# The opening of a four-layer kernel on one core: matmuls that nobody reads, rows issued by two engines, shared weights in half pieces

## Chip, cores and metric

The program runs on one core of a Trainium2 chip. The metric is the device time of one execution in microseconds. All 16 sequences of the batch are computed in one launch.

## The reference

Sixteen sequences x of 256 tokens and 256 features go through four residual layers:

```python
x = x + linear(x, weight[subject], bias[subject])                  # L0
x = x + zX * lap_x(x) + zY * lap_y(x) + zR * x * (1 - x)           # L1, 3-point differences, mirrored edges
x = x + attention(x, side, length)                                 # L2
x = x + expert_mix(x, label)                                       # L3
```

L2 has 16 heads of 16 features. Its queries come from a second sequence `side`, the keys and values from x (masked by a length), and each query has one more score and value, its own, from `side`; an output projection Wo follows. L3 runs three two-layer ReLU networks of width 1024 on all tokens: two shared ones (`swi`, `swo`) and one chosen by the label (`wi`, `wo`). Their outputs are added with softmax weights that a small gate network computes from the first token.

## The kernel before

**Engines and lists.** Each engine runs its own program. What it does in which order is written out by hand as a list of names; a name such as `S3` or `kp` is a stage, and semaphores bind the stages of different engines together. `PE_BODY`, `ACT_BODY`, `DVE_BODY`, `POOL_BODY` and `SP_BODY` are one turn of the loop over sequences. A turn works on several sequences at once: the scores of one (`S`, `E`), the early layers of the next, and the experts (`H`, `P`) of the one before. `OPEN_PE`, `OPEN_ACT`, `OPEN_DVE`, `OPEN_POOL` and `OPEN_SP` (lines 114 to 135) are the opening, which fills this pipeline: it carries sequence 0 up to the experts' input and through its 16 heads, and sequence 1 (names ending in `.1`) up to its rows. Then the loop starts.

**Precision.** Values in fp32 are split into a high part (ScalarE copies it to the matmul's format) and a low part (the rest, subtracted by VectorE or GpSimd). A product is three matmuls: high with high, high with low, low with high (lines 631 to 633). A 256 by 256 projection is 12 matmuls of 128 by 128 weights and 256 columns. For the scores, q and k are split into three bf16 parts each, and copied by DMA into `q_rows` and `k_rows`, where the parts of one head lie stacked on the partitions: six bands of 16 rows each for q and for k, 128 KB per band, and a mask row that comes from memory (`place`, line 481). TensorE then gets a head's score in one product.

**The stages by name.** `x1` is L0 (12 matmuls with the subject's weight, which SP loads after it has read the subject number); `x1_parts` splits its result, `beside` (in the stage `x1` of GpSimd, line 1334) adds the two neighbours of each token, `react` is the reaction term, `lap` the difference along features (four matmuls with `lap_mats`), `x2_parts` splits the result of L1. `q`, `kp`, `ks`, `vs`, `vp`, `self` are the projections of the side sequence and of x with three of the four matrices of `wqkvo` (in `raw`, split by `lin0` to `lin3` into `lin_hi` and `lin_lo`) and the own scores. `qa`, `qb`, `kq`, `k3` make the second and third parts. `S0` to `S15` compute the scores of a head with queries on the partitions, only to find their maxima (VectorE, line 1125). `m0` and `m1` turn the maxima of eight heads round, and a DMA puts them into `q_rows` (line 516). `E0` to `E15` compute the scores again with keys on the partitions; ScalarE takes two exponentials of each (lines 966 and 970), VectorE or GpSimd makes the low part (1145, 1378), and TensorE multiplies with the values three heads later (`attend`, lines 693 and 694). `half`, `norm` and `att` divide the sums, `aT` transposes them, `wo` is the output projection. `H` and `P` are steps of the two expert layers. The S and E heads and the projections share two PSUM banks in the order in which they are listed, so a stage waits until the one two places ahead in the list has been read.

**The shared weights.** `swi` and `swo` are 4 MB in eight pieces of 512 KB. Each has to be loaded to a place that is free, split into `exp_hi` by ScalarE and into `exp_lo` by VectorE (pieces 0 and 1) or GpSimd (2 to 7), and its place can then be used again. The places are written in one list:

```python
STAGES = ["e_out", "gate1", "raw0", "raw1", "e_out", "gate1", "e_out", "gate1"]
```

Pieces 4 and 5 therefore wait for the split of 0 and 1, pieces 6 and 7 for that of 4 and 5, which in the opening's lists comes late. The gate's own weights go to `gate1` after that.

**Warm matmuls.** Before the first load has landed, TensorE runs 16 matmuls on `q_rows` that nobody reads (`warm`, line 845), after VectorE has set `q_rows`.

## Time and profile before

| | before |
|---|---|
| time, median of 3 runs | 1043.14 us (1041.8 to 1044.29) |
| the profiled execution's own time | 1044.92 us |
| its span in the profile | 1043.1 us |
| TensorE busy | 979.5 us (94%) |
| VectorE busy | 777.6 us (75%) |
| ScalarE busy | 688.6 us (66%) |
| GpSimd busy | 618.6 us (59%) |

Times in the profile are microseconds from the start of the span. PE is TensorE, PEld its weight loads, DVE is VectorE, ACT ScalarE, POOL GpSimd, SPq the sequencer of SyncE that issues DMAs. A line number is one of the kernel's. "<-" behind idle time names what ended it. The granted clock is TensorE's, as a share of 2.4 GHz. The end of a matmul is modelled, so the pace of a series of matmuls is read from their starts.

### The profile page before, as it was taken

What the parts mean: (1) busy time and instruction counts of PE and PEld (TensorE: products, weight loads), DVE (VectorE), ACT (ScalarE), POOL (GpSimd) and SP (SyncE); (2) the same over time, 40 slices, a digit from 0 to 9 for tenths busy, and PEclk for the clock granted to TensorE, in tenths of its full rate; (3) what the DMA queues carried; (4) which work ended last, traced back from release to release, by engine and by line L of the source; (5) the groups of instructions that cost most, each with busy time, mean ns of one, the idle gap of its engine ahead of it and who ended that gap; (6) DMA issues with size and microseconds to landing.
All of it is one profiled execution on the core that took longest, in us unless ns stands there. A gap on an engine that the chain in (4) does not pass through costs nothing.

```text
span 1043.1 us, 27678 instructions
## 1 busy us (share of the span) xinstructions
PE 979.5 (94%) x9504; PEld 921.1 (88%) x9504; DVE 777.6 (75%) x1553; ACT 688.6 (66%) x1435; POOL 618.6 (59%) x545
## 2 busy tenths in 40 slices
PE   7567999999999999999999999999999999999886
PEld 6256999999999999899999999999999999999886
DVE  5755778787877878787787878778777878778643
ACT  4365676858667685867767586776768587676641
POOL 4467566747565664756576575657657565665540
PEclk9567999999999999999999999999999999999998
DMA  5515343152425325142522514342341524243110
GB/s 145 148 42 109 95 90 94 45 115 63 61 82 97 85 56 117 51 71 81 91 81 66 113 44 85 87 70 81 76 106 41 102 81 61 81 87 66 43 51 11
DMA packets 91387, 82.68 MB, mean 79 GB/s; under 512 B 11972, under 2 KB 90852, under 8 KB 91364
## 3 DMA queue, kind: packets, MB, share of 16 engines
q1 hardware_dynamic: 91364, 82.38, 34.5%
q8 instruction: 14, 0.23, 0.1%
q14 instruction: 9, 0.07, 0.0%
HBM read 52.59 MB, written 4.20 MB: 54 GB/s over the span
## 4 chain that ended last, share of the span: by engine, by line
PE 58%; issue 11%; DVE 8%; ACT 7%; SPq 6%; POOL 6%; DMA 4%; ACTq 0%; DVEq 0%; POOLq 0%
PE out L631 6%; PE out L632 6%; PE out L633 6%; PE hid L631 5%; PE front L751 5%; PE hid L632 4%; PE hid L633 4%; PE front L631 4%; PE front L633 4%; PE front L632 4%; PE front L738 3%; DMA raw<-in_wo 3%; PE pv L693 3%; PE pv L694 2%; ACT prob_hi L970 2%
## 5 line engine op out<-in xcount | busy, mean ns | idle before, releaser
L1378 POOL TENSOR_TENSOR prob_lo<-prob,prob_hi 128x512 f16<-128x512 f32 x144 | 173.4, 1204 | 115.3 <-ACT prob_hi L970 115.3
L631 PE MATMUL hid<-x_hi,exp_hi 128*128 128x256 f32 x768 | 230.7, 300 | 2.0 <-DVE x_lo L1205 2.0
L631 PE MATMUL out<-hid_hi,exp_hi 128*128 128x256 f32 x768 | 227.3, 296 | 4.1 <-DVE hid_lo L1209 3.5
L632 PE MATMUL hid<-x_lo,exp_hi 128*128 128x256 f32 x768 | 216.6, 282 | 0.0
L633 PE MATMUL hid<-x_hi,exp_lo 128*128 128x256 f32 x768 | 215.9, 281 | 0.0
L632 PE MATMUL out<-hid_lo,exp_hi 128*128 128x256 f32 x768 | 214.9, 280 | 0.0
L633 PE MATMUL out<-hid_hi,exp_lo 128*128 128x256 f32 x768 | 214.7, 280 | 0.0
L1317 POOL TENSOR_TENSOR exp_lo<-raw,exp_hi 128x512 fp32r<-128x512 f32 x128 | 169.8, 1342 | 68.4 <-ACT exp_hi L986 68.4
L1125 DVE TENSOR_REDUCE s_max<-front 128x2 f32<-128x512 f32 x256 | 168.9, 687 | 53.4 <-PE front L738 51.2
L966 ACT ACTIVATE prob<-front 128x512 f32<-128x512 f32 x256 | 153.4, 600 | 51.0 <-PE front L751 51.0
L1008 ACT ACTIVATE hid_hi<-hid 128x512 fp32r<-128x512 f32 x192 | 114.6, 597 | 106.1 <-PE hid L633 104.3
L1209 DVE SCALAR_TENSOR_TENSOR hid_lo<-hid,hid_hi 128x512 fp32r<-128x512 f32 x192 | 130.5, 680 | 52.3 <-ACT hid_hi L1008 50.1
L631 PEld LDWEIGHTS out<-hid_hi,exp_hi 128*128 128x128 f32 x768 | 144.8, 188 | 8.1 <-DVE hid_lo L1209 4.2
L631 PEld LDWEIGHTS hid<-x_hi,exp_hi 128*128 128x128 f32 x768 | 145.1, 189 | 4.7 <-DVE x_lo L1205 2.2
L632 PEld LDWEIGHTS hid<-x_lo,exp_hi 128*128 128x128 f32 x768 | 145.5, 189 | 0.0
L632 PEld LDWEIGHTS out<-hid_lo,exp_hi 128*128 128x128 f32 x768 | 145.2, 189 | 0.0
L633 PEld LDWEIGHTS hid<-x_hi,exp_lo 128*128 128x128 f32 x768 | 144.9, 189 | 0.0
L633 PEld LDWEIGHTS out<-hid_hi,exp_lo 128*128 128x128 f32 x768 | 144.6, 188 | 0.0
L970 ACT ACTIVATE prob_hi<-front 128x512 f16<-128x512 f32 x240 | 143.8, 599 | 0.0
L751 PE MATMUL front<-q_rows,k_rows 100*128 100x256 bf16 x512 | 125.2, 280 | 11.3 <-ACT prob_hi L970 7.6
L1145 DVE TENSOR_TENSOR prob_lo<-prob,prob_hi 128x512 f16<-128x512 f32 x112 | 92.6, 827 | 17.0 <-ACT prob_hi L970 16.0
L738 PE MATMUL front<-k_rows,q_rows 97*128 97x256 bf16 x512 | 90.6, 285 | 13.2 <-DVE s_max L1125 7.0
(174 smaller groups left out, 2273.1 us busy)
## 6 DMA issues: line engine op xcount, KB each, us to landing
raw<-in_wi SPq DMA_DIRECT2D x64, 256.0 KB, 3.5
raw<-in_wo SPq DMA_DIRECT2D x64, 256.0 KB, 2.9
q_rows<-w_raw SPq DMA_DIRECT2D x80, 128.0 KB, 3.6
k_rows<-x1T SPq DMA_DIRECT2D x48, 128.0 KB, 4.4
k_rows<-x_raw SPq DMA_DIRECT2D x48, 128.0 KB, 5.5
x_raw<-in_x SPq DMA_DIRECT2D x16, 256.0 KB, 2.9
s_raw<-in_side SPq DMA_DIRECT2D x16, 256.0 KB, 3.7
w_raw<-in_w SPq DMA_DIRECT2D x16, 256.0 KB, 2.8
```

The costliest lines, as they stand in the source:

```text
L631: nc.tensor.matmul(acc, w_hi, a_hi, start=first, stop=False)
L632: nc.tensor.matmul(acc, w_hi, a_lo, start=False, stop=False)
L633: return nc.tensor.matmul(acc, w_lo, a_hi, start=False, stop=last)
L738: last = nc.tensor.matmul(psum[:, t * S:(t + 1) * S], q_rows[0:ROWS_MAX, h, t * P:(t + 1) * P], k_rows[0:ROWS_MAX, h, :], start=True, stop ...
L751: last = nc.tensor.matmul(psum[:, k * S:(k + 1) * S], k_rows[0:ROWS_EXP, h, k * P:(k + 1) * P], q_rows[0:ROWS_EXP, h, :], start=True, stop ...
L966: last = nc.scalar.activation(prob[:, h % NPROB, :], psum[:, :], ACT.Exp, scale=SCALE)
L970: last = nc.scalar.activation(prob_hi[:, h % NPROB, :], psum[:, :], ACT.Exp, scale=SCALE)
L1008: nc.scalar.activation(hid_hi[:, s % 2, :], hid_bank[s % 2][:, :], ACT.Relu).then_inc(hid_hi_done, 1)
L1125: nc.vector.tensor_reduce(s_max[:, :, h:h + 1], psum, AX_X, ALU.max).then_inc(freed["S"], 1)
L1209: nc.vector.scalar_tensor_tensor(hid_lo[:, s % 2, :], hid_bank[s % 2][:, :], 0.0, hid_hi[:, s % 2, :].bitcast(F32), ALU.max, ALU.subtract) ...
L1317: nc.gpsimd.tensor_tensor(lo, source, hi.bitcast(F32), ALU.subtract).then_inc(w_split, 1)
L1378: nc.gpsimd.tensor_tensor(prob_lo[:, h % NPROB, :], prob[:, h % NPROB, :], prob_hi[:, h % NPROB, :], ALU.subtract).then_inc(prob_split_poo ...
```

## The change

The loop's lists stay as they are. In the opening:

- TensorE's list gets 19 `fill` entries, 93 matmuls of 256 columns with `lap_mats` into `hid1`, which nobody reads; `warm` has 20 matmuls instead of 16, reads `v_cols` and so waits for GpSimd's first memset instead of VectorE's. E0 to E3 move in between S13, S14 and S15, x1.1 and m1 move later.
- The first k copies (`k0`, three DMAs) are issued by ScalarE instead of SP; SP's order becomes q0, q1, mask row, q2, k1, k2.
- The first loads go out as subject, x, w0, small, s instead of x, subject, s, w0, small.
- A shared piece is loaded, and split, in two halves of 256 KB, each with its own place; there are ten such places (x3T, x3_kept and the ends of e_out and gate1 are new). Pieces 2 and 3 are loaded ahead of load.1, 4 to 7 right behind m0. VectorE splits three pieces (0, 1, 5), GpSimd five. The matmuls in H0, H4, P0, P4 and P8 wait for the counts that this gives, by constants; that is three waits more per sequence.
- lin0 to lin3 are all split by GpSimd, in halves, with one semaphore. `beside` of sequence 0 is VectorE's. k3 goes ahead of shared0 on VectorE, and GpSimd waits for the first half's maxima (`maxima`) before it splits the inputs of sequence 1. The other lists are rearranged to fit.

```diff
 OPEN_PE = list(opening("""
-warm x1 bias_q lap q bias_k kp ks vs vp self
-S0 S1 S2 S3 S4 S5 S6 S7 S8 m0 S9 S10 S11 S12 S13 S14 S15 E0 E1 m1 x1.1 E2 E3 E4 E5 E6 q.1 E7 lap.1 E8 E9 E10 E11 kp.1 E12 E13 E14 E15
-pvend vs.1 aT ks.1 wo vp.1 self.1
+warm x1 bias_q fill14 lap q bias_k kp ks vs vp self fill4
+S0 S1 fill4 S2 S3 fill4 S4 S5 fill4 S6 S7 S8 fill10 m0 S9 S10 fill4 S11 S12 fill8 E0 E1 S13 S14 fill2 E2 E3 S15 x1.1 E4 fill3 E5 fill3
+m1 E6 q.1 E7 fill3 lap.1 E8 fill3 E9 fill3 E10 fill3 E11 kp.1 E12 fill3 E13 fill3 E14 fill3 E15 fill6
+pvend vs.1 fill6 aT ks.1 wo vp.1 self.1
 """))
 OPEN_ACT = list(opening("""
-x_parts s_parts w_parts lin0 x1_parts react lin1 lin2 x2_parts q qa lin3 shared0 kp qb kq ks shared1 vs vp x2b
-w_parts.1 x_parts.1 s_parts.1 m0 shared2 E0 E1 m1 shared3 E2 x1_parts.1 react.1 E3 E4 E5 E6 q.1 E7 qa.1 E8 x2_parts.1 E9 E10 E11 kp.1
-E12 E13 E14 E15 qb.1 kq.1 shared4 aT vs.1 ks.1 shared5 x3_parts vp.1 x2b.1 shared6 shared7
+x_parts w_parts s_parts lin0 x1_parts react lin1 lin2 x2_parts q qa lin3 kp qb k0 kq ks vs shared0 vp shared1 x2b
+shared2 shared3 w_parts.1 x_parts.1 m0 s_parts.1 E0 E1 E2 E3 E4 E5 m1 x1_parts.1 react.1 E6 q.1 E7 shared4 qa.1 E8 x2_parts.1
+E9 E10 E11 kp.1 E12 E13 E14 E15 qb.1 kq.1 shared5 shared6 aT vs.1 ks.1 shared7 x3_parts vp.1 x2b.1
 """))
 OPEN_DVE = list(opening("""
-memsets x_lo s_lo w_lo laps x_parts x1 lin0 x1_parts bias_q react lap x2_parts setup bias_k kp shared0 k3 vp self shared1
-S0 S1 S2 S3 S4 S5 S6 S7 S8 S9 S10 S11 S12 x_parts.1 S13 S14 S15 x1.1 E1 x1_parts.1 react.1 E3 E5 lap.1 E7 x2_parts.1 half E11 kp.1
-E13 E15 att k3.1 aT wo x3_parts vp.1 self.1
+memsets x_lo w_lo s_lo laps x_parts x1 beside x1_parts react bias_q lap setup x2_parts bias_k kp k3 shared0 vp self shared1
+S0 S1 S2 S3 S4 S5 S6 S7 S8 S9 S10 S11 S12 x_parts.1 S13 S14 E1 S15 x1.1 E3 x1_parts.1 react.1 E5 E7 lap.1 x2_parts.1 half E11 kp.1
+E13 E15 att k3.1 aT shared5 wo x3_parts vp.1 self.1
 """))
 OPEN_POOL = list(opening("""
-memsets x1 lin1 lin2 qa lin3 qb ks vp w_parts.1 x_parts.1 s_parts.1 shared2 E0 x1.1 E2 shared3 E4 E6 m1 E8 E9 qa.1 E10 E12 norm E14
-qb.1 shared4 ks.1 shared5 vp.1 shared6 shared7
+memsets lin0 lin1 qa lin2 qb ks vp lin3 shared2 maxima w_parts.1 x_parts.1 s_parts.1 E0 E2 x1.1 shared3 E4 E6 m1 E8 shared4 E9 qa.1
+E10 E12 norm E14 qb.1 ks.1 vp.1 shared6 shared7
 """))
 OPEN_SP = list(opening("""
-mask q0 k0 q1 k1 mask_row q2 k2 load.1 shared2 shared3 shared4 shared5 m0 m1 wi_load E15 kp.1 k3.1 shared6 shared7 gates
+mask q0 q1 mask_row q2 k1 k2 shared2 shared3 load.1 m0 shared4 shared5 shared6 shared7 m1 wi_load E15 kp.1 k3.1 gates
 """))
...
-STAGES = ["e_out", "gate1", "raw0", "raw1", "e_out", "gate1", "e_out", "gate1"]
+STAGES = [("e_out", 0, 1), ("gate1", 0, 1), ("raw", 0, 1), ("x3", 0, 1), ("raw", 2, 3), ("ends", 0, 1), ("e_out", 0, 1), ("gate1", 0, 1)]
 SHARED = len(STAGES)
-SHARED_DVE = 2
+SHARED_DVE = 3
...
-WARM = 16
+WARM = 20
...
             def load_shared(n):
...
+                e, part = n // 4, n % 2
+                for m, dest in enumerate(staged(n)):
+                    if n % 4 < 2:
+                        columns = slice(m * F // 2, (m + 1) * F // 2)
+                        sp.dma_start(dest, swi[e, part * P:(part + 1) * P, columns]).then_inc(shared_in[n], 16)
+                    else:
+                        chunks = F // 4
+                        at = slice((2 * part + m) * chunks, (2 * part + m + 1) * chunks)
+                        sp.dma_start(dest.rearrange("p (f d) -> p f d", d=D),
+                                     swo[e, at].rearrange("(f p) d -> p f d", p=P)).then_inc(shared_in[n], 16)
...
-                    wait(sp, w_split, PARTS, i, 4 - SHARED_DVE if isinstance(i, int) and i == 0 else SHARED_POOL)
+                    wait(sp, w_split, PARTS, i, 3 if isinstance(i, int) and i == 0 else SHARED_POOL)
...
+            sp.dma_start(subject_sb[:, :], subject).then_inc(choice_in, 16)
             load_x(0)
-            sp.dma_start(subject_sb[:, :], subject).then_inc(choice_in, 16)
-            load_s(0)
             sp.wait_ge(choice_in, 16)
             load_w0(chooser(subject_sb, 0, w0.shape[0]))
             load_small(0, chooser(subject_sb, 0, w0.shape[0]))
+            load_s(0)
...
                 if s == 0:
                     wait(pe, x3_split, 1, j, 1)
+                    pe.wait_ge(shared_split_dve, 2)
+                elif s == STEPS:
                     pe.wait_ge(shared_split_dve, SHARED_DVE)
-                    pe.wait_ge(w_split, 4 - SHARED_DVE)
-                elif s == STEPS:
-                    pe.wait_ge(w_split, SHARED_POOL)
+                    pe.wait_ge(w_split, 4)
...
                 if s == 0:
                     wait(pe, logits_read, 1, j, 1)
+                    pe.wait_ge(w_split, 2)
                 elif s % STEPS == 0:
                     wait(pe, e_out_done, NE, j, e)
+                    pe.wait_ge(w_split, SHARED_POOL)
...
-                pe.wait_ge(q_rows_set, 1)
+                pe.wait_ge(rows_set, 1)
+                plane = v_cols[:, 0, :, :].rearrange("p h w -> p (h w)")
                 for _ in range(WARM):
-                    nc.tensor.matmul(front_bank[0][:, 0:S], q_rows[0:ROWS_MAX, 0, 0:P], q_rows[0:ROWS_MAX, 1, :], start=True, stop=True)
+                    nc.tensor.matmul(hid_bank[1][:, 0:S], plane[:, 0:P], plane[:, 0:S], start=True, stop=True)
+
+            def fill(count):
+
+                pe.wait_ge(consts_set, 1)
+                for _ in range(count):
+                    nc.tensor.matmul(hid_bank[1][:, 0:S], lap_mats[:, 0:P], lap_mats[:, :], start=True, stop=True)
...
+                elif name == "k0":
+                    act.wait_ge(rows_set, 3)
+                    act.wait_ge(k_part_done, C)
+                    place(act, k_rows, K_BANDS, k_parts, 0, k_placed)
...
+                elif name == "beside":
+                    dve.wait_ge(freed["x1"], 1)
+                    ends = x1T[:, :, 1:S - 1:S - 3]
+                    nc.vector.tensor_tensor(beside[:, :, 1:S - 1], x1T[:, :, 0:S - 2], x1T[:, :, 2:S], ALU.add)
+                    nc.vector.tensor_tensor(beside[:, :, 0:S:S - 1], ends, ends, ALU.add).then_inc(beside_done, 1)
...
+                elif name == "wo":
+                    dve.wait_ge(w_split, 2)
+                    stage(name, seq)
...
+                elif name == "maxima":
+                    pool.wait_ge(max_split, 1)
```

## Rows read from the trace of the kernel before

**Rows 1.** Stretches of the whole run; columns: busy time and count by engine, granted clock, DMA.

```profile
0.00:55.00 55.00, 36.65 (x170) 26.17 (x170) 32.83 (x64) 22.08 (x41) 23.57 (x23) 0.78 0.51 139
55.00:110.00 55.00, 40.33 (x331) 34.94 (x330) 30.46 (x52) 31.32 (x60) 38.59 (x33) 0.72 0.45 102
...
170.00:1043.00 873.00, 843.33 (x8412) 803.53 (x8410) 667.66 (x1343) 592.67 (x1245) 519.13 (x457) 1.00 0.33 75
```

**Rows 2.** The chain of waits in order of time, its start: start us, us, what.

```profile
1.22 2.32 DMA subject_sb<-in_subject
...
4.51 2.66 DMA w_raw<-in_w
```

**Rows 3.** Timeline of TensorE: start us, us, what, idle time before it.

```profile
14.62 0.55 PE L716 MATMUL front<-x_hi,lap_mats 128*128 128x256 f32 x1 [1.60 <-DVE x_lo L1069]
...
16.46 0.41 PE L632 MATMUL front<-s_lo,lin_hi 128*128 128x256 f32 x1
16.68 0.41 PE L633 MATMUL front<-s_hi,lin_lo 128*128 128x256 f32 x1
...
18.17 1.70 PE L841 MATMUL pv<-vec_sb,raw 128*128 128x2 f32 x8
...
24.25 0.28 PE L631 MATMUL front<-s_hi,lin_hi 128*128 128x256 f32 x1
24.37 0.28 PE L632 MATMUL front<-s_lo,lin_hi 128*128 128x256 f32 x1
```

**Rows 4.** Timeline of SP's DMA queue: first k0 copy group, last row copy.

```profile
23.65 1.83 SPq L485 DMA_DIRECT2D k_rows<-x1T  x3
...
30.79 0.60 SPq L485 DMA_DIRECT2D k_rows<-x_raw  x1
```

**Rows 5.** The chain of waits, the last row copy's way.

```profile
30.79 3.96 DMA k_rows<-x_raw
```

**Rows 6.** Stretch in which the last row copies move.

```profile
30.00:32.00 2.00, 0.00 (x0) 0.00 (x0) 1.12 (x1) 0.00 (x0) 2.00 (x2) 0.73 1.06 138
```

**Rows 7.** Timeline of TensorE, VectorE and ScalarE in the S heads.

```profile
34.99 1.01 PE L738 MATMUL front<-k_rows,q_rows 97*128 97x256 bf16 x4 [6.23 <-DMA k_rows<-x_raw]
...
35.61 5.48 DVE L1125 TENSOR_REDUCE s_max<-front 128x2 f32<-128x512 f32 x8 [4.49 <-PE front L738]
...
41.33 1.14 DVE L1134 TENSOR_SCALAR m_parts<-s_max 128x16 bf16<-128x16 f32 x1
...
49.63 0.60 ACT L966 ACTIVATE prob<-front 128x512 f32<-128x512 f32 x1 [4.68 <-PE front L751]
```

**Rows 8.** Stretches: S heads, then E heads.

```profile
34.99:50.50 15.51, 10.86 (x38) 2.76 (x38) 13.35 (x29) 4.18 (x8) 6.24 (x5) 0.50 0.60 187
49.50:82.00 32.50, 21.92 (x204) 16.44 (x204) 16.53 (x30) 22.89 (x46) 21.81 (x19) 0.66 0.14 42
```

**Rows 9.** Groups of instructions by line, 34.99 to 81.60 us.

```profile
L966 ACT ACTIVATE prob<-front 128x512 f32<-128x512 f32 x16 | 9.7, 606 | 10.2 <-PE front L751 10.2
```

**Rows 10.** Timeline of GpSimd, VectorE and TensorE around att.

```profile
82.36 2.57 POOL L1310 TENSOR_TENSOR exp_lo<-e_out,exp_hi 128x512 fp32r<-128x512 f32 x2 [0.32 <-ACT exp_hi L980]
...
83.13 1.95 DVE L1172 TENSOR_TENSOR att<-att,v_self 128x128 f32<-128x128 f32 x2
...
85.67 1.11 PE L659 MATMUL pv<-ident,att 128*128 128x128 f32 x4 [1.34 <-DVE att L1175]
```

**Rows 11.** Timeline of ScalarE and TensorE before P0.

```profile
98.04 1.06 ACT L980 ACTIVATE exp_hi<-gate 128x1024 fp32r<-128x1024 f32 x1 [2.12 <-DMA gate<-in_swo]
...
100.36 0.58 PE L631 MATMUL out<-hid_hi,exp_hi 128*128 128x256 f32 x1 [3.48 <-DVE hid_lo L1209]
```

**Rows 12.** Stretch from P0 on.

```profile
100.40:106.30 5.90, 5.90 (x28) 5.59 (x28) 2.99 (x5) 1.23 (x3) 3.76 (x4) 0.52 0.54 156
```

**Rows 13.** Timeline of TensorE: first two products after P1's wait.

```profile
106.68 0.36 PE L631 MATMUL out<-hid_hi,exp_hi 128*128 128x256 f32 x1
106.88 0.28 PE L632 MATMUL out<-hid_lo,exp_hi 128*128 128x256 f32 x1
```

More of the change, by code:

```diff
@@ L172, in in_place @@
 def in_place(name, i):
[L174 removed]
+    orders = {1: ("w_parts", "x_parts", "s_parts")}
     order = orders[i] if isinstance(i, int) and i in orders else ("x_parts", "w_parts", "s_parts")
@@ L426, in staged, with halves_of_piece @@
         def staged(n):
-            size = C * F // 2
-            whole = {"e_out": e_out[:, :, :, :].rearrange("p e c t -> p (e c t)"), "gate1": gate1[:, :, :].rearrange("p k f -> p (k f)"),
-                     "raw0": raw, "raw1": raw[:, size:2 * size]}
-            return whole[STAGES[n]][:, 0:size]
+            flat_e, flat_g = e_out[:, :, :, :].rearrange("p e c t -> p (e c t)"), gate1[:, :, :].rearrange("p k f -> p (k f)")
+            halves = {"e_out": [flat_e[:, m * 512:(m + 1) * 512] for m in range(2)], "gate1": [flat_g[:, m * 512:(m + 1) * 512] for m in range(2)],
+                      "raw": [raw[:, m * 512:(m + 1) * 512] for m in range(4)],
+                      "x3": [t[:, :, :].rearrange("p c t -> p (c t)") for t in (x3T, x3_kept)],
+                      "ends": [flat_e[:, 1024:1536], flat_g[:, 1024:1536]]}
+            kind, first, second = STAGES[n]
+            return halves[kind][first], halves[kind][second]
+        def halves_of_piece(n):
+            at, half = shared_piece(n), C * F // 4
+            return [slice(at.start + p * half, at.start + (p + 1) * half) for p in range(2)]
         def expert_w(part, e):
@@ L437, in expert_w, with place @@
             return w_in, w_out
+        def place(eng, rows, bands, parts, n, done):
+            for band, part in enumerate(bands):
+                if part == n:
+                    eng.dma_start(rows[band * DH:(band + 1) * DH, :, :], parts[n]).then_inc(done, 16)
         block = ctx.enter_context(nc.Block())
@@ L859, in _ @@
                     warm()
+                elif name[0:4] == "fill":
+                    fill(int(name[4:]))
                 elif name == "bias_q":
@@ L977, in shared_hi_part @@
             def shared_hi_part(n):
-                at = shared_piece(n)
-                act.wait_ge(shared_in[n], 16)
-                nc.scalar.activation(exp_hi[:, n // 4, at], staged(n), ACT.Copy).then_inc(shared_hi, 1)
+                act.wait_ge(shared_in[n], 32)
+                for at, source in zip(halves_of_piece(n), staged(n)):
+                    last = nc.scalar.activation(exp_hi[:, n // 4, at], source, ACT.Copy)
+                last.then_inc(shared_hi, 1)
             def chosen_hi_part(n, j):
@@ L1305, in split_shared @@
             def split_shared(n):
-                at, half = shared_piece(n), C * F // 4
                 pool.wait_ge(shared_hi, n + 1)
-                for p in range(2):
-                    part = slice(at.start + p * half, at.start + (p + 1) * half)
-                    last = nc.gpsimd.tensor_tensor(exp_lo[:, n // 4, part], staged(n)[:, p * half:(p + 1) * half],
-                                                   exp_hi[:, n // 4, part].bitcast(F32), ALU.subtract)
+                for at, source in zip(halves_of_piece(n), staged(n)):
+                    last = nc.gpsimd.tensor_tensor(exp_lo[:, n // 4, at], source, exp_hi[:, n // 4, at].bitcast(F32), ALU.subtract)
                 last.then_inc(w_split, 1)
@@ L1320, in lin_lo_part @@
                 pool.wait_ge(lin_hi_done, n + 1)
-                nc.gpsimd.tensor_tensor(lin_lo[:, n, :], raw[:, n * C * D:(n + 1) * C * D], lin_hi[:, n, :].bitcast(F32), ALU.subtract
-                                        ).then_inc(lin_split_pool, 1)
+                for k in range(C):
+                    part = slice(k * D, (k + 1) * D)
+                    last = nc.gpsimd.tensor_tensor(lin_lo[:, n, part], raw[:, n * C * D + k * D:n * C * D + (k + 1) * D],
+                                                   lin_hi[:, n, part].bitcast(F32), ALU.subtract)
+                last.then_inc(lin_split, 1)
             def stage(name, i):
```

80 lines of the change are left out of this document (29 added, 51 removed).

## The prediction

> **What bounds the kernel now.** I read the stretch view first. From 170 us to the end TensorE is busy 843 of 873 us at granted clock 1.00, so the loop is bound by TensorE. From 55 to 110 us it is busy 40 of 55 us at granted clock 0.72 [rows 1]. The change leaves the loop lists alone, so whatever it gives or costs must arise before about 110 us and then be carried through the loop to the end. The other views were therefore read for the first 110 us alone.
>
> The chain of waits begins with a serial load: the subject number is fetched, and only then can w_raw, whose address depends on it, be issued [rows 2]. The timeline of TensorE shows its clock. Products of 256 columns follow each other by 0.22 us at 16.46 and 16.68, which is the 1.2 GHz level, and by 0.12 us at 24.25 and 24.37, the 2.4 GHz level; so early I go by spacing. The rise comes after dense products since 19.9 us (18.17 + 1.70), behind the one-or-two-column bias products of row 18.17 [rows 3].
>
> Next come the rows. SP issues twelve copies of 128 KB and a mask row. The three k0 copies hold it 1.83 us, q1 follows, and the last copy is issued at 30.79 [rows 4] and lands 3.96 us later [rows 5]. TensorE has waited 6.23 us when S0 starts at 34.99 [rows 7].
>
> In the S heads VectorE paces: eight reductions take 5.48 us back to back, and a 16-column m_parts takes 1.14 us [rows 7] while GpSimd splits the next inputs. The granted clock is 0.50 there, and in the E heads 0.66, where ScalarE is busy 22.89 and GpSimd 21.81 of 32.5 us: nobody is full, the stretch is a chain of small waits [rows 8]. ScalarE waits 10.2 us in it for E products [rows 9]. After E15, VectorE's two additions to att take 1.95 us beside a GpSimd shared split [rows 10]. Last, TensorE waits 3.48 us for hid_lo [rows 11] because ScalarE splits shared piece 7 only at 98.04, after 2.12 us of waiting for its load, which had to wait for its place to come free, and the 5.9 us after that run at clock 0.52 [rows 12].
>
> **Part by part, with the working.** Negative is time saved.
>
> 1. *Start.* Subject goes out ahead of x: 0.50 us earlier, so w_raw and x1 come 0.5 earlier [rows 2]. x's landing is not late, since w_raw lands last. Side moves behind the small loads; only q needs it, 6 us later. The four more warm matmuls cost nothing: x1 waits for w_raw.
>
> 2. *x1 to kp.* Lap began at 14.62 after a wait of 1.60 us [rows 3]. Fill14 is placed in that wait, but at 1.2 GHz it is 14 x 0.22 = 3.1 us and ends near 15.6, so lap is about 1.0 late. In exchange dense work runs unbroken from 12.5, and I put the rise inside q (about 17.5) instead of 24. From there bias_k and kp take 1.0 and 1.4 us instead of 1.7 and 2.6. The sum moves kp's end from 22.4 to about 21.0: -1.4, the 0.5 of point 1 in it. Moving beside to VectorE puts some 0.9 us ahead of x1_parts, lin0 leaves the engine for 0.68; lin0, lin1 are done by GpSimd by 15.2: hidden. If the rise stays out, lap's delay remains: +0.5.
>
> 3. *Rows.* k0's 1.83 us leave SP [rows 4] and go to ScalarE, where kq (and so k1, k3, k2) stands behind them; SP meanwhile issues q1, mask row and q2. VectorE does k3 ahead of shared0 now. My list gives the last issue at 26.2 instead of 30.8. The copies cannot follow: six that were queued together moved at 138 GB/s with the DMA engines full [rows 6], 0.95 us each. I let them land at 31.7 instead of 34.75: -3.0 in all up to S0, point 2 included (bounds -1.4 and -4.5). Shared 2 and 3 now go out right behind k2 and ahead of load.1; they queue behind the rows on the same queue. load.1 then queues behind one megabyte, but x1.1 needs it only some 14 us after S0. The mask row is bound as before to its wait for the stored mask, which is over by then.
>
> 4. *S and E heads.* S heads stay at VectorE's 0.685 [rows 7]; four fills at 0.12 fit beside two reductions (1.37 us), at 0.21 they don't (0.85 + 0.85 = 1.7). "maxima" keeps GpSimd off until m_parts is made: about -0.9. E0 to E3 are mixed into S13 to S15, so ScalarE starts E0 10.8 us after S0 (S0 to S11 and m_parts on VectorE 9.1, fill8 1.0, E0's products and releases 0.7; its maxima, 12 KB issued at 7.5, must land by 10) instead of 14.6 [rows 7]. From there its own list (32 exponentials of 0.6 [rows 9], plus inputs, q, kp, shared4) would end E15 some 8 us earlier, GpSimd's list 7.4 earlier. Three blocks of 12 products (x1.1, q.1, kp.1) take 1.4 instead of 2.6 us where the clock holds. The fills there, 27 in threes, are 0.36 us each time and lie in waits if the predecessor is late, else on the path. Between -2 (the early E0 is eaten by the chain) and -8 I take -5.5: the lists are not full, but every wait in them stays.
>
> 5. *att, aT, wo.* Shared4 is split ahead of norm, so the 1.95 us additions [rows 10] come near 0.6: -1.2 (0 to -1.5). ks.1 and wo at full clock save 1.0, VectorE's shared5 between aT and wo gives half back: -0.5 (0 to -1).
>
> 6. *The wait before P0.* Pieces 6 and 7 have places long before, ScalarE reaches H0 in time, and P0 follows S1: -3.4 [rows 11]. Late next are GpSimd's splits of 6 and 7 (2.57 us each [rows 10]), which H4 and P4 need only 10 us on. The 5.9 us at clock 0.52 go to full clock: -2.7 [rows 12].
>
> 7. *Waits in the loop.* hidden and project wait on constants three times more per sequence, 48 in all. After a wait the second product starts 0.20 instead of 0.12 us later [rows 13]; so 0 to 48 x 0.08 = 3.8 us, and below nothing is excluded. The values are long reached and TensorE's queue runs ahead: +0.5.
>
> Sum: -3.0 - 5.5 - 1.2 - 0.5 - 3.4 - 2.7 + 0.5 = -15.8. The profiled execution took 1044.92 us (span 1043.1), 1.78 over the median of 1043.14. 1044.92 - 15.8 = 1029.1, and against the median 1027.3.
>
> **The rivals.**
> *A. The rows are bound by the transfers.* Nine copies after kp at 0.95 us [rows 6] from 22.5 on land near 33.3: points 1 to 3 give 1.4 instead of 3.0. For it: the full engines at 30 us. Against: k0's copies before them left gaps while SP was held. Time 1028.9; chance 0.15. The Trainium skill, DMA: Bandwidth & Descriptors, section Issuing engines are not separate DMA queues, says copies started by several engines share the same 16 DMA engines, so only issue time is saved; the full engines of rows 6 agree with that rule.
>
> *B. The clock does not stay up.* Fills keep TensorE busy only where they are; in the row wait of 3 us and in the E heads, where each fill is short, it falls as before. Fills then lie in waits, but points 4 to 6 lose their clock part (1.5, 0.5, 0) and point 4 half the rest: -15.8 + 5.3. Time 1032.6; chance 0.18. For it: granted clock 0.66 with TensorE busy 21.9 of 32.5 us [rows 8].
>
> *C. The lists fill up.* Point 4 gives 8.0, S0 comes 4.5 earlier, att 1.5: 4.3 more. Time 1023.0; chance 0.22. For it: GpSimd and ScalarE each have a third of idle time in the E heads.
>
> *D. Slower: the fills are the path.* There are 93 of them in the opening (the counts behind "fill" in the list). At 0.213 us they are 19.8 us, and if the clock stays low all of it stands ahead of products that are ready. What needs no clock (P0's wait 3.4, att 1.2, rows 2.0, early E heads 2.0) is 8.6. Net +11.2: 1054.3. It decides from 8.6 / 0.213 = 40 such fills on. Against: ScalarE waits 10.2 us for E products in this stretch [rows 9], and VectorE paces the S heads, so many fills have room; chance 0.07.
>
> *E. Nothing is carried over.* The opening is shorter but the loop then waits for loads at its first turns until the old schedule returns. TensorE's 97% in the loop speaks against it: 1043; chance 0.03.
>
> **Numbers.** The forecast's own case has 0.35. The range 1018 to 1037 holds A, B, C and the bounds of point 4, and leaves out D, E and the tails. A difference under 0.2% (2.1 us) can't be told from none. Faster 0.90, same 0.03, slower 0.07.
>
> **What would show it.** S0's first product near 31.7 us (35.0 before); aT near 76.0 (85.67 [rows 10]); P0 near 86.8 (100.36 [rows 11]) straight behind S1 with no wait over 1 us; granted clock at 0.8 or more from 35 to 110; TensorE's share in the loop unchanged. Wrong would be: S0 later than 34, fills with a ready successor for over 8 us, VectorE idle between reductions of S heads, or a loop turn that is longer than before.

## The result and the profile after

The changed kernel takes 1038.97 us (median; 1037.4 to 1041.67), the kernel before in the same runs 1044.94 us (1041.8 to 1046.8). The ratio is 0.9948, with a 95% interval of 0.9937 to 0.9958: faster by 0.5%, or 6.0 us, where 15.8 were forecast, and outside the range of 1018 to 1037. The profiled execution took 1038.21 us, its span is 1036.4 us.

The page of the changed kernel, part 1 (busy time, share, count):

```profile
PE 978.4 (94%) x9601; PEld 924.9 (89%) x9601; DVE 780.8 (75%) x1558; ACT 688.3 (66%) x1443; POOL 610.1 (59%) x546
```

TensorE is busy 1.1 us less and runs the 97 added matmuls. Its stretches, columns as in [rows 1]:

```profile
0.00:55.00 55.00, 38.39 (x252) 32.16 (x253) 32.02 (x70) 24.84 (x49) 25.46 (x28) 0.82 0.65 158
55.00:110.00 55.00, 45.66 (x424) 40.68 (x422) 37.98 (x64) 35.04 (x75) 37.43 (x33) 0.93 0.44 97
...
170.00:1036.00 866.00, 835.66 (x8341) 795.99 (x8339) 663.19 (x1330) 586.60 (x1233) 510.04 (x454) 0.99 0.33 74
```

TensorE works more in both opening stretches, at a higher clock than in [rows 1]; in the loop it is as full as before (96.5%).

The milestones, in us from the span's start, read from the timelines:

| first instruction of | before | after | ahead | forecast ahead |
|---|---|---|---|---|
| kp on TensorE | 19.73 | 17.25 | 2.5 | 1.4 (its end) |
| S0 on TensorE | 34.99 | 33.18 | 1.8 | 3.0 |
| E0 on ScalarE | 49.63 | 45.35 | 4.3 | |
| kp.1 on TensorE | 70.94 | 68.49 | 2.5 | |
| E15 on ScalarE | 79.11 | 77.18 | 1.9 | 8.5 |
| aT | 85.67 | 82.28 | 3.4 | 9.7 |
| x3T, first sequence | 90.69 | 86.27 | 4.4 | |
| P0 | 100.36 | 91.94 | 8.4 | 13.6 |
| P1 | 106.68 | 95.69 | 11.0 | 16.3 |
| x3T, second sequence | 156.81 | 148.18 | 8.6 | |
| aT of the last sequence | 991.20 | 983.95 | 7.3 | 15.8 |
| end of the span | 1043.1 | 1036.4 | 6.7 | 15.8 |

The forecast's 8.5 at E15 is 3.0 + 5.5. Two things stand out: the lead hardly grows between S0 and E15, where the largest term was, and 4.3 us of it are given back after P1.

**The rows.** The chain of waits of the changed kernel, then its stretches while the copies move:

```profile
24.28 8.66 DMA k_rows<-x_raw
32.94 0.25 issue
33.18 1.01 PE front L745 x4
```

```profile
22.00:24.00 2.00, 1.10 (x9) 0.90 (x9) 0.76 (x2) 2.00 (x6) 0.51 (x1) 1.00 1.13 112
24.00:26.00 2.00, 2.00 (x19) 2.00 (x18) 1.03 (x2) 1.75 (x5) 0.78 (x1) 1.00 1.16 120
...
30.00:32.00 2.00, 0.00 (x0) 0.00 (x0) 0.00 (x0) 0.00 (x0) 1.25 (x2) 0.50 1.13 132
```

The last row copy is issued 6.5 us earlier than in [rows 4], and takes 8.66 us where it took 3.96 [rows 5]. From 22 us on the DMA engines are full, at 112 to 132 GB/s (the share counts the time that packets take, so it can pass 1).

**The S heads.** Timeline of TensorE (with the fills) and of VectorE:

```profile
33.18 1.01 PE L745 MATMUL front<-k_rows,q_rows 97*128 97x256 bf16 x4 [6.65 <-DMA k_rows<-x_raw]
33.85 1.20 PE L865 MATMUL hid<-lap_mats 128*128 128x256 f32 x4
34.85 1.08 PE L745 MATMUL front<-k_rows,q_rows 97*128 97x256 bf16 x4
```

```profile
35.54 1.29 DVE L1148 TENSOR_REDUCE s_max<-front 128x2 f32<-128x512 f32 x2 [0.45 <-PE front L745]
...
40.54 0.17 DVE L1157 TENSOR_SCALAR m_parts<-s_max 128x16 bf16<-128x16 f32 x1
```

Four fills take 0.85 to 1.0 us, which is the 1.2 GHz level. A pair of heads takes 1.73 us, and VectorE now waits 0.45 us before each pair; in [rows 7] it reduced eight heads back to back. The m_parts operation takes 0.17 us (1.14 in [rows 7]) now that GpSimd waits for it.

**The E heads.** Timelines of GpSimd and VectorE:

```profile
55.95 1.27 POOL L1333 TENSOR_TENSOR exp_lo<-x3T,exp_hi 128x512 fp32r<-128x512 f32 x1
57.17 1.30 POOL L1333 TENSOR_TENSOR exp_lo<-x_kept,exp_hi 128x512 fp32r<-128x512 f32 x1
58.43 3.19 POOL L1403 TENSOR_TENSOR prob_lo<-prob,prob_hi 128x512 f16<-128x512 f32 x2
...
66.74 2.96 POOL L1333 TENSOR_TENSOR exp_lo<-raw,exp_hi 128x512 fp32r<-128x512 f32 x2
69.66 1.16 POOL L1403 TENSOR_TENSOR prob_lo<-prob,prob_hi 128x512 f16<-128x512 f32 x1
```

```profile
57.67 1.36 DVE L1092 TENSOR_TENSOR x_lo<-x1T,x_hi 128x512 fp32r<-128x512 f32 x1 [2.72 <-ACT x_hi L940]
58.95 1.64 DVE L1111 TENSOR_TENSOR react<-react,x1T 128x512 f32<-128x512 f32 x1
```

Two shared pieces are split among the heads, and the low parts of heads stand behind them on GpSimd. Piece 3 stood there before the change too (3.38 us); piece 4 is new. VectorE's operations beside them are long. The lead over the kernel before, by ScalarE's first exponential of a head, shows where it goes: 4.3 us at E0, 5.0 at E7 (60.62 against 65.57), 2.9 at E8 (64.45, 67.34), 3.5 at E12 (71.54, 75.03) and 1.9 at E13 (75.25, 77.18). The chain of waits of the changed kernel ahead of E8 and ahead of E13 runs through VectorE:

```profile
58.95 1.65 DVE react L1111
60.62 1.55 DVE react L1113
62.20 1.44 DVE prob_lo L1168
...
71.20 1.03 DVE prob_hi L1167
72.25 1.52 DVE prob_lo L1168
```

**The clock.** With the fills it is up in the S heads, where it was 0.50 before, and higher behind 55 us; e1 below is the kernel without them. Stretches of the changed kernel, then of e1:

```profile
35.00:50.00 15.00, 11.78 (x79) 8.17 (x77) 10.26 (x23) 7.37 (x16) 7.86 (x7) 0.84 0.54 170
```

```profile
35.00:50.00 15.00, 10.66 (x46) 3.03 (x45) 10.86 (x24) 7.70 (x16) 8.50 (x7) 0.50 0.59 185
```

From 55 to 110 us it is 0.93 in the changed kernel, 0.84 in e1 and 0.72 before.

**P0**, timeline of TensorE: behind S1 without a wait, where [rows 11] has 3.48 us.

```profile
91.58 0.61 PE L745 MATMUL front<-k_rows,q_rows 97*128 97x256 bf16 x4
91.94 0.36 PE L638 MATMUL out<-hid_hi,exp_hi 128*128 128x256 f32 x1
```

### The profile page after: what moved, and what is told of

Same layout as the page of the kernel before. It is cut to its first block, busy times and chain, and to the rows that moved or that the text cites. A ratio compares the mean times of both kernels' runs of the same rounds, so it can differ in the third digit from the quotient of the medians.

```text
span 1036.4 us, 27927 instructions
## 1 busy us (share of the span) xinstructions
PE 978.4 (94%) x9601; PEld 924.9 (89%) x9601; DVE 780.8 (75%) x1558; ACT 688.3 (66%) x1443; POOL 610.1 (59%) x546
## 4 chain that ended last, share of the span: by engine, by line
PE 55%; issue 13%; DVE 8%; ACT 8%; SPq 6%; POOL 5%; DMA 4%; ACTq 0%; DVEq 0%; POOLq 0%
PE out L638 5%; PE out L640 5%; PE out L639 5%; PE front L758 5%; PE hid L638 4%; PE hid L639 4%; PE hid L640 4%; PE front L638 4%; PE front L640 4%; PE front L639 4%; DMA raw<-in_wo 3%; PE front L745 3%; ACT prob_hi L988 3%; PE pv L700 2%; PE pv L701 2%
## 5 line engine op out<-in xcount | busy, mean ns | idle before, releaser
L1148 DVE TENSOR_REDUCE s_max<-front 128x2 f32<-128x512 f32 x256 | 169.0, 687 | 54.2 <-PE front L745 52.5
L1168 DVE TENSOR_TENSOR prob_lo<-prob,prob_hi 128x512 f16<-128x512 f32 x112 | 96.2, 860 | 15.8 <-ACT prob_hi L988 14.8
L745 PE MATMUL front<-k_rows,q_rows 97*128 97x256 bf16 x512 | 88.2, 280 | 14.5 <-DMA k_rows<-x_raw 6.7
```

Of the source, the lines that this page charges most:

```text
L745: last = nc.tensor.matmul(psum[:, t * S:(t + 1) * S], q_rows[0:ROWS_MAX, h, t * P:(t + 1) * P], k_rows[0:ROWS_MAX, h, :], start=True, stop ...
L1148: nc.vector.tensor_reduce(s_max[:, :, h:h + 1], psum, AX_X, ALU.max).then_inc(freed["S"], 1)
```

## The experiments

Each run is told with its ratio to the kernel before, its interval, and the milestones that the theories differ in. One caution holds for all: the changed kernel profiled twice (e11) differs by up to 0.6 us at the milestones up to P1 and by 0.9 us at the second x3T, S0 lies between 33.08 and 33.74 us in kernels with nearly the same work ahead of it, and e12, whose opening up to E15 is that of e9, by up to 1.3 us (E8: 63.54 and 62.26). So a difference under about 1 us at one milestone is not read by itself.

**e1 and e2: the fills.** TensorE's opening list has 20 `fill` entries with the 93 matmuls. Both runs take out the 19 behind lap; e1 takes out fill14 too.

```diff
-warm x1 bias_q fill14 lap q bias_k kp ks vs vp self fill4
-S0 S1 fill4 S2 S3 fill4 S4 S5 fill4 S6 S7 S8 fill10 m0 S9 ...
+warm x1 bias_q lap q bias_k kp ks vs vp self
+S0 S1 S2 S3 S4 S5 S6 S7 S8 m0 S9 ...
```

> The changed kernel without its 93 fill matmuls (the 20 warm ones stay). Theory A (fills pay): between x1 and the rows the clock falls back to 1.2 GHz, kp ends 1 us or more later, the S and E heads lose their stretches at 2.4 GHz, H0 starts later; ratio to the kernel before about 0.998, that is 3 to 4 us above the changed kernel. Theory B (fills are neutral): the stretches that they warm are bound by VectorE, ScalarE and GpSimd anyway, and the three fill4 blocks at 1.2 GHz that stood ahead of ready S heads (1.1 us) are saved; ratio 0.994 to 0.995, within 1 us of the changed kernel.

> The changed kernel with fill14 ahead of lap as its only fill. Theory A: the gain up to kp is kept (S0 near 33.2 us), the loss in the S and E heads as without any: 2 to 3 us above the changed kernel. Theory B: same as the changed kernel or 1 us faster, since S0 to S7 take 6.1 us again instead of 7.1, and E heads are as fast.

e1: 1036.64 us, ratio 0.9943 (0.9929 to 0.9956). e2: 1036.48 us, 0.9938 (0.9925 to 0.9952). Neither can be told from the changed kernel (0.9937 to 0.9958): the fills are worth nothing here, although they do raise the clock. In e1 VectorE has its eight reductions back to back again:

```profile
33.74 5.47 DVE L1148 TENSOR_REDUCE s_max<-front 128x2 f32<-128x512 f32 x8 [3.14 <-PE front L745]
```

E0 comes at 44.31 (45.35 with fills), aT at 81.89 (82.28), P0 at 92.04 (91.94). The fills cost 1.0 us in the S heads, and at P0 nothing is left of it. kp starts at 17.27 without fill14 and at 17.25 with it: lap starts 1.1 us earlier without (12.74 and 13.86), and most of q and bias_k then run at 0.21 us spacing and take that back. Kp itself also runs at 0.21 us without it, so its last product is 1.2 us later, but S0 is not (33.12 and 33.18).

**e3: are the row copies slowed by shared pieces 2 and 3, which now stand right behind them on the queue?** The pieces go behind load.1; ScalarE splits them behind the inputs of sequence 1, and GpSimd splits piece 2 behind `maxima`, to fit.

```diff
-mask q0 q1 mask_row q2 k1 k2 shared2 shared3 load.1 m0 ...
+mask q0 q1 mask_row q2 k1 k2 load.1 shared2 shared3 m0 ...
```

> The changed kernel with the loads of shared pieces 2 and 3 (1 MB) behind load.1 instead of ahead of it, so that nothing shares the DMA engines with the last row copies. Theory A (the shared loads slow the rows): the last row copy takes 5 us or less instead of 8.7, S0 starts near 30 us, 3 us earlier, ratio about 0.992. Theory B (the copies are bound by their own rate, some 130 GB/s): S0 stays within 0.7 us of 33.2 and the ratio stays near 0.995.

1037.3 us, 0.9955 (0.9942 to 0.9969), S0 at 33.19 (33.18). The last row copy still takes 8.40 us (8.66). The loads behind them do not slow the rows.

**e5: does the second issuer help?** k0 goes back to SP, between q0 and q1.

```diff
-mask q0 q1 mask_row q2 k1 k2 ...
+mask q0 k0 q1 mask_row q2 k1 k2 ...
```

> The changed kernel with the three k0 copies issued by SP again, between q0 and q1, all else as changed. Theory A (the copies are bound by the DMA engines): the last copy is issued 1.5 to 2 us later but lands within 0.5 us of 32.9, S0 near 33.2, the time of the changed kernel. Theory B (issue counts): S0 1.5 us or more later and the time 1 to 2 us longer, ratio 0.996.

1039.6 us, 0.9981 (0.9968 to 0.9993). S0 starts at 33.09, although the last copy leaves over 3 us later. The chain of waits of e5:

```profile
28.05 4.79 DMA k_rows<-x_raw
32.84 0.25 issue
33.09 1.01 PE front L749 x4
```

With e3 this shows the core of rival A: S0 is set by the transfers, which end at the same time, whoever issues them. It is not a plain full queue, though: in e5 the share of the DMA engines is only 0.57 from 25 to 28 us, and then the copies move at 184 GB/s at a share of 0.80. Copies that are queued together take more of the engines' time each; why is not shown. The ratio of e5 is 0.3% over that of the changed kernel, and the intervals do not meet. The difference does not come from the opening, whose second x3T (147.39) is earlier than the changed kernel's (148.18); the 13 turns of the loop take 60.38 us each where the changed kernel has 60.29, which is 1.2 us in all. Why, and where the rest lies, is not settled; so the second issuer is shown to be worth nothing for S0, and not for the whole time.

**e4: the input split of sequence 1 earlier** on ScalarE.

```diff
-... E0 E1 E2 E3 E4 E5 m1 x1_parts.1 react.1 E6 q.1 ...
+... E0 E1 E2 E3 E4 x1_parts.1 react.1 E5 m1 E6 q.1 ...
```

> The changed kernel with ScalarE's x1_parts.1 and react.1 right behind E4 instead of behind E5 and m1. Theory A (the E heads' lead of 4 us at E4 was lost because VectorE's x_lo waited 2.7 us for this split, with the react chain and the low parts of E5 and E7 behind it): E15 about 1.5 us earlier, ratio about 0.993 to 0.994. Theory B (the lead is lost to the low clock and to GpSimd's port): E15 moves by less than 0.5 us, ratio 0.995.

1036.61 us, 0.9943 (0.993 to 0.9957). VectorE's x_lo starts at 55.58 instead of 57.67, but E15 stays at 77.17 and aT at 82.17. The chain of waits of e4 passes through GpSimd instead:

```profile
56.33 3.48 POOL exp_lo L1333 x2
59.81 1.57 POOL prob_lo L1403
```

VectorE's wait alone was not what holds the E heads.

**e6: E heads behind the S heads again**, with m1, x1.1 and its splits in their old order, without fills, so the comparison is with e1.

```diff
-... S11 S12 E0 E1 S13 S14 E2 E3 S15 x1.1 E4 ...
+... S11 S12 S13 S14 S15 E0 E1 m1 x1.1 E2 E3 E4 ...
```

> The kernel without fills with S13 to S15 ahead of E0 again, and m1, x1.1, x1_parts.1 and react.1 in the old order among the E heads. To be read against the run without fills. Theory A (mixing E0 to E3 into the S heads brings the 1.5 to 2 us of lead that is left at E15): aT 1.5 us later or more and the time up by that. Theory B (what the mixing gains is lost by x1.1 and its split coming later): E0 starts 3.5 us later but aT moves by less than 0.7 us, time within 1 us.

1037.73 us, 0.9962 (0.995 to 0.9973). E0 comes at 47.00 (44.31 in e1), aT at 83.53 (81.89), P0 at 93.85 (92.04). But S0 is 0.6 us later too (33.74 and 33.12), which this edit cannot have caused. Counted from S0, the early E0 to E3 give 2.1 us at E0, of which 1.0 is left at aT; the ratios differ by 0.0019, and their intervals overlap.

**e7: pieces 6 and 7 late**, as before: loaded behind k3.1, split by ScalarE at its list's end.

```diff
-... m0 shared4 shared5 shared6 shared7 m1 wi_load E15 kp.1 k3.1 gates
+... m0 shared4 shared5 m1 wi_load E15 kp.1 k3.1 shared6 late7 gates
```

> The changed kernel with shared pieces 6 and 7 loaded late again: 6 behind k3.1, 7 after ks.1, and ScalarE splits both behind x2b.1 as before the change. The theory that the gain comes from the places: TensorE waits 2.5 to 4 us before P0, the stretch behind it runs partly at 1.2 GHz, the lead at the second x3T falls by 4 us, ratio 0.998 to 0.999. The rival (the first turn of the loop absorbs it, since it has slack elsewhere): P0 late by 3 us, but the second x3T late by 1 us or less, ratio 0.995.

1041.57 us, 0.9993 (0.9982 to 1.0003): nearly the whole gain is gone. aT is as in the changed kernel (82.67), and the wait is back, longer than the 2.5 to 4 us expected. Timeline of TensorE in e7:

```profile
98.57 0.58 PE L642 MATMUL out<-hid_hi,exp_hi 128*128 128x256 f32 x1 [5.71 <-DVE hid_lo L1236]
98.95 0.41 PE L643 MATMUL out<-hid_lo,exp_hi 128*128 128x256 f32 x1
99.16 0.41 PE L644 MATMUL out<-hid_hi,exp_lo 128*128 128x256 f32 x1
```

P0 is 6.6 us later than in the changed kernel, and the products behind it have the 0.21 us spacing of 1.2 GHz. At the second x3T it is 6.4 us; in the time it is 0.0045 of the ratio, or 4.7 us.

**e8: what GpSimd's splits cost among the E heads.** The low parts of pieces 3 and 4 are cut to 8 columns of each half; the rest of these low parts is zero, so part of the experts' product is left out.

```diff
             def split_shared(n):
...
+                    if n in (3, 4):
+                        at, source = slice(at.start, at.start + 8), source[:, 0:8]
```

> The changed kernel with GpSimd's low parts of shared pieces 3 and 4 cut to 8 columns of each half (the rest of them is set to zero at the start, so two pieces of the experts' weights lose their low part): 5 us of GpSimd work leave the E heads. Theory A (GpSimd and its reads beside VectorE's hold the E heads): E8 to E15 1.5 to 3 us earlier, aT near 80, time 1.5 to 3 us less than the changed kernel. Theory B (the chain of E, exponentials, low parts and projections at 1.2 GHz holds them): aT moves by less than 0.7 us.

1033.16 us, 0.992 (0.9899 to 0.9941). E15 comes at 72.58 (77.18) and aT at 77.57 (82.28), 4.7 us earlier, for splits that take 1.2 us instead of 5.5. Of this 0.7 us was there before the first of these splits (E4 at 53.52 and 54.25), so 4.0 belong to them. The ratio shows 3 us; the profiled span is 7.5 us shorter, but it is that of the fastest of four executions. GpSimd's splits are what bounds the E heads. VectorE's operations beside them shrink too; timeline of VectorE in e8:

```profile
56.53 0.72 DVE L1092 TENSOR_TENSOR x_lo<-x1T,x_hi 128x512 fp32r<-128x512 f32 x1 [2.32 <-ACT x_hi L940]
57.24 0.69 DVE L1111 TENSOR_TENSOR react<-react,x1T 128x512 f32<-128x512 f32 x1
```

The same two took 1.36 and 1.64 us beside the splits. The run takes away both GpSimd's time and what the splits cost VectorE, so it does not say which of the two is worth more. The chains above have VectorE's stretched operations on the path in the changed kernel, and GpSimd's own split in e4, where VectorE is early. The granted clock from 50 to 70 us rises too, from 0.67 to 0.91.

**e9, e10 and e11: the splits moved instead of cut.** Piece 3 is split by GpSimd before the first maxima, 4 by VectorE behind aT, 5 by GpSimd behind ks.1; wi_load goes behind k3.1 and waits accordingly. e9 is without fills, e10 with them; e11 is the changed kernel again, measured beside them.

```diff
-memsets lin0 ... lin3 shared2 maxima w_parts.1 ... x1.1 shared3 E4 E6 m1 E8 shared4 E9 qa.1
-E10 E12 norm E14 qb.1 ks.1 vp.1 shared6 shared7
+memsets lin0 ... lin3 shared2 shared3 maxima w_parts.1 ... x1.1 E4 E6 m1 E8 E9 qa.1
+E10 E12 norm E14 qb.1 ks.1 shared5 vp.1 shared6 shared7
```

> The kernel without fills, with GpSimd's 5 us of low parts taken out of the E heads: piece 3 ahead of maxima, where GpSimd idles, piece 4 to VectorE behind aT in place of piece 5, piece 5 on GpSimd behind ks.1, and the first load of wi behind k3.1 (it waits for piece 4). If GpSimd holds the E heads: aT near 78 instead of 81.9 and the time 3 to 4 us under the run without fills, ratio 0.990 to 0.992. What may take it back: wi lands late behind the rows, so that ScalarE stands at wi0 with H1's result behind it, 1 to 2 us. If the rival holds (what helped was only work left out, and it costs the same elsewhere): ratio 0.994.

> The same edit on the changed kernel with its 93 fills. Theory A (fills are neutral whatever bounds the E heads): within 1 us of the run before this one. Theory B (with GpSimd out of the way the projections at 1.2 GHz become the bound, and fills then pay): 1.5 us or more faster than the one without.

> The changed kernel itself once more, beside the two above on the same chip. If fills are neutral its ratio is that of the run without fills, 0.994 to 0.995. The second question is the turn of the loop, 60.3 us against 60.1 us of the kernel before in its first profile though the lists are the same: if that belongs to the kernel it comes again, if it is chance the turn is 60.1 to 60.2.

e9: 1036.6 us, 0.9917 (0.99 to 0.9935). e10: 1035.13 us, 0.9904 (0.9886 to 0.9922). e11: 1040.16 us, 0.9949 (0.9931 to 0.9967). aT comes at 78.35 in e10 against 82.67 in e11, with all splits done, and the intervals of the two are apart: what e8 showed by leaving work out is to be had by moving it. The run without fills to set beside e9 is e1: aT 79.92 against 81.89, and ratios 0.9917 and 0.9943, whose intervals just overlap. Whether the fills add something to e10 is open (the intervals of e9 and e10 overlap). The second question of e11, whether the longer loop turn belongs to the kernel, got a yes by its own measure: 60.28 us again.

**e12: why the first loop turn gives back lead.** The changed kernel loses 2.4 us of lead between P1 and the second x3T (2.6 in e11), most of it in three waits. Timeline of TensorE after P1:

```profile
101.93 0.28 PE L751 MATMUL front<-ident_half,m_parts 128*24 128x128 bf16 x2 [1.06 <-DVE m_parts L1160]
...
107.78 0.39 PE L758 MATMUL front<-q_rows,k_rows 100*128 100x256 bf16 x2 [0.42 <-DMA q_rows<-max_rows]
...
110.57 0.39 PE L745 MATMUL front<-k_rows,q_rows 97*128 97x256 bf16 x2 [0.52 <-DVE s_max L1148]
```

The kernel before has no wait there. VectorE and GpSimd of the changed kernel before the first of them:

```profile
98.94 2.22 DVE L1155 SCALAR_TENSOR_TENSOR s_max<-s_max,s_self 128x16 f32<-128x16 f32 x1
```

```profile
96.10 5.03 POOL L1339 TENSOR_TENSOR exp_lo<-raw,exp_hi 128x512 fp32r<-128x512 f32 x4
```

A 16-column operation takes 2.22 us and ends with GpSimd's fourth split. e12 is e9 with GpSimd held until the maxima are made:

```diff
-E10 E12 norm E14 qb.1 ks.1 shared5 vp.1 shared6 shared7
+E10 E12 norm E14 qb.1 ks.1 shared5 vp.1 shared6 shared7 maxima.1
```

> The kernel e9 with one wait more: GpSimd's opening list ends with maxima.1, so the four wi splits of the first loop turn (5.02 us from 94.44 in e9) start only when VectorE has made the first half's m_parts of sequence 1. Theory (the first turn gives back lead because these splits hold VectorE's 128x16 s_max operation, 1.02 us in e9 and 2.22 us in the changed kernel, where undisturbed ones take 0.17): that operation takes 0.17 us, TensorE's wait for m_parts at about 100 (0.88 us in e9) is gone, and the stretch from aT to the second sequence's x3T, 65.93 us in e9, is 0.8 to 1.0 us shorter; the end comes as much earlier, 1.0 us of 1036. Rival (the list is late by itself): s_max takes 0.17 but TensorE waits as long in another place of the turn, because the splits now come late for the expert products or the low parts of E heads behind them: the stretch stays at 65.9 or is longer.

1035.92 us, 0.9922 (0.9909 to 0.9936), as e9. The s_max operation takes 0.17 us, and so does the m_parts one behind it, which took 1.21 us in e9 with a single tensor as input. The wait for m_parts is gone. But the next wait, in e9 0.36 us, has grown; timeline of TensorE in e12:

```profile
105.78 0.39 PE L760 MATMUL front<-q_rows,k_rows 100*128 100x256 bf16 x2 [1.23 <-DMA q_rows<-max_rows]
```

The E product starts where it did in e9 (105.84), and from P0 to the second x3T it is 55.87 us against 55.57. By the expected measure, from aT, it is 65.65 against 65.93, where 0.8 to 1.0 us less were expected. The rival was right that the wait only changes its place, though its reason (splits late for what stands behind them) was not the one. Late is SP's copy of max_rows: in e12 they are made by 99.9 us, and the copy leaves at 103.01. In the changed kernel ScalarE has made them by 102.7; the queue of SP:

```profile
96.21 0.40 SPq L594 DMA_DIRECT2D gate<-in_g  x1
96.65 0.55 SPq L595 DMA_DIRECT2D gate<-in_g  x1
98.28 0.39 SPq L469 DMA_DIRECT2D w_raw<-in_w  x1
...
102.57 2.80 SPq L482 DMA_DIRECT2D raw<-in_wo  x3
105.51 0.87 SPq L527 DMA_DIRECT2D q_rows<-max_rows  x1
```

Here the copy stands 2.8 us behind loads. The queue is late from its entry gates on, and the waits of SP say for what:

```profile
SPq L593 <- POOL exp_lo L1333: 10.7, 1, 10.7
```

The gate's weights go to a place whose shared piece GpSimd splits last (piece 7, ending at 96.13). Before, the same two gate loads left at 101.72 and 102.13, so this queue is only 5.5 us ahead where TensorE at P1 is 11.0 ahead; there the copy of max_rows left at 112.60, as soon as it was made. That a copy ahead of these loads, or a gate place that comes free earlier, would keep the 2 us was not tried.

## Why the prediction was wrong, point by point

The direction and the place were right: all of the gain arises before P1. Its size was a bit more than a third of the forecast. The step that failed is the one in point 4 that took the lists of ScalarE and GpSimd in the E heads as work to be packed: 5.5 us were forecast from S0 to E15, and 0.1 came, because GpSimd's splits of shared pieces bound this stretch (e8, e10). By the prediction's own steps:

**Points 1 and 2** (-1.4). Better than forecast: kp starts 2.5 us earlier, and its end, which the forecast is for, comes 3.7 us earlier (18.76 against 22.44). Most of it is the start. x1 starts at 6.94 instead of 8.60, and its products have the 0.12 us spacing of 2.4 GHz where they had 0.21: 1.7 and 1.1 us, against 0.5 forecast. The 0.5 counted only the earlier issue of subject; its way to the landing also shrank, from 2.32 us [rows 2] to 1.19, issue included. The warm matmuls begin at 2.18 us instead of 3.04. Fill14 did what was forecast (lap 1.1 us late, the rise inside q, at 15.3), and its 1.2 us at the end of kp did not reach S0, as e1 shows.

**Point 3** (-3.0 up to S0): -1.8. As points 1 and 2 gave 2.3 us more than forecast, the rows themselves are 3.5 us short. The step that failed here is "I let them land at 31.7": 32.94 was measured. From the first row copy's issue to the last one's landing it is 14.7 us in both kernels (20.05 to 34.75, and 18.20 to 32.94), so the new order of issue won nothing. At 112 to 132 GB/s a queued copy took 1.0 to 1.2 us, not 0.95. Rival A named this mechanism and 33.3 us, but its own working, nine copies at 0.95 us from 22.5 on, ends at 31.05; the number was partly luck. The Trainium skill, DMA: Bandwidth & Descriptors, section Issuing engines are not separate DMA queues, says that a second issuer saves issue time only; e5 agrees, with S0 at 33.09 from one issuer and 33.18 from two.

**Point 4** (-5.5): -0.1 from S0 to E15. This is the term that failed, and the largest part of the miss. Its first half came true in part: E0 is 4.3 us ahead, 2.5 of them behind S0 (mixing gives 2.1 by e6, what is left without it 1.4, the free m_parts above all, and the fills take 1.0 by e1). All of it is lost until E15, in two places, ahead of E8 and of E13. The step "ScalarE's own list would end E15 some 8 us earlier, GpSimd's 7.4" took the lists as work to be packed, and counted shared4, which the change puts among the E heads, as an entry that has room. e8 shows the contrary: 4.3 us less of splits on GpSimd are 4.0 to 4.7 us at aT. The splits act in two ways. They stretch VectorE's operations beside them (1.64 us for react, 0.69 in e8), which stand on the chain of waits ahead of E8 and E13; the forecast knew this from [rows 10] and priced it only for att. And an E head's low part waits behind each split on GpSimd, so that TensorE cannot attend and the ring of two banks stops ScalarE; that is the chain in e4. How much each is worth was not separated. That GpSimd was busy 21.8 of 32.5 us [rows 8] did not mean that it had 10 us for the taking: its waits there were for exponentials (3.28, 2.21 and 2.72 us) and for x1.1 (3.72 us). That a split fits into such waits without delaying the next head was assumed, and e8 and e10 show that it did not.

**The fills** were taken as free at 0.12 us. In the first S heads they were not: four of them took over 0.85 us, the case that point 4 warned of ("at 0.21 they don't" fit), and VectorE stood idle between its reductions, one of the forecast's own signs of being wrong. Then they did raise the clock. From 35 to 110 us it is 0.88 (0.66 before, 0.75 in e1), so the sign "0.8 or more" came true, and from 70 to 110 us it does not fall again, where in e1 it is at 0.50 from 77.5 to 80. Yet e1 takes the same time: TensorE's pace was not what bounded these stretches. So rival B's premise held only in part (from 50 to 70 us the clock is 0.67 in both kernels); its sum does not come out either (1.5 + 0.5 and half of the remaining 4.0 of point 4 are 4.0, not 5.3). D did not come. The fills fell mostly into waits.

**Point 5** (-1.7): -2.5 from E15 to x3T. The additions to att take 0.62 us instead of 1.95 [rows 10], as forecast; timeline of VectorE:

```profile
81.08 0.62 DVE L1195 TENSOR_TENSOR att<-att,v_self 128x128 f32<-128x128 f32 x2
```

**Point 6** (-6.1): -6.6 from x3T to P1, the one large term that was right in mechanism and in size. e7 shows it: with the two pieces late, P0 is 6.6 us late. Its sentence on what is late next was incomplete. It named H4 and P4 as the readers of pieces 6 and 7; the third reader is the place itself, for which SP's gates wait with the whole queue of the first turn behind them (e12).

**Point 7** (+0.5): the loop turns average 60.29 us against 60.19, which is 1.3 us in 13 turns; but kernels with the same loop lists have 60.06 (e6) to 60.38 (e5), so the waits cannot be charged with it. The changed kernel itself has 60.28 again in e11; what sets the turn is open. What the point missed is the first turn, which gives back 2.4 us. That was rival E's mechanism, there for one turn and not for all.

Behind the last aT 0.6 us more go. The sum as measured: -1.8 - 0.1 - 2.5 - 6.6 + 2.4 + 1.3 + 0.6 = -6.7, the difference of the spans. Against the forecast 1.2 of the missing 9.1 us lie in points 1 to 3, 5.4 in point 4, 3.8 in the loop and behind it (4.3 measured, 0.5 forecast), and points 5 and 6 give 1.3 back.

## What to carry to other kernels

An engine at two thirds busy inside a chain of small waits need not have a free third: before a job is put there, ask which short operation will stand behind it and which operations of other engines run beside it, and put it where the next customer is far away (e10 against e11: the same splits, three places elsewhere, 0.45% of the time). S0 was bound by transfers, and a second issuer did not move it; look at the bandwidth of the stretch before counting issue slots. A clock that has risen is worth nothing where another engine sets the pace (e1). When a buffer's split goes later than its neighbours', list every reader of its place, the next load into it and what stands in that queue among them.
